# Second attention layer of a two-layer vision tower: gate shares from ScalarE's sigmoid, their products on GpSimd, a five-op cumulative step on VectorE

## What is computed

```
q, k, v, u = X @ Wq.T, X @ Wk.T, X @ Wv.T, X @ Wu.T          # per head
gate = X @ Wg.T                                               # per head: 3 numbers, two are used
s_i = -sum(u * (log_tau * prior_mu + cumsum(u)) / (log_tau + t)) / sqrt(d)
E_t = cumsum(exp(s_i - max(s_i)));  P_t = cumsum(s_i)
F_t, G_t, H_t = cumsum(exp_s * kv), cumsum(s_i * kv), cumsum(kv)
sig1, sigh = sigmoid(gate[0]), sigmoid(gate[1])
alpha = sigh / (E_t + 1e-12)
beta  = (sig1 - sigh) / t
gamma = -((beta * P_t + sigh) / t)
out = q @ (alpha * F_t + beta * G_t + gamma * H_t)            # then a layer norm per head, then Wo
```

## Time and profile before

| | |
|---|---|
| median of 3 runs | 573.85 us (572.05 to 574.06) |
| the profiled execution's own time | 573.22 us |
| its span, first to last instruction | 571.4 us |
| busy: PE / DVE / ACT / POOL | 519.4 / 382.5 / 255.6 / 225.8 us |
| mean granted clock of PE | 0.949 |

### The profile page before, as it was taken

One profiled execution on the slowest core, in us unless ns is written; L12 is line 12 of the kernel. 1 busy time (PEld: TensorE's weight loads), 2 busy tenths in 40 slices (PEclk: granted clock), 3 DMA queues, 4 the chain that ended last, 5 costly groups with the idle time before them and its releaser, 6 DMA issues.

```text
span 571.4 us, 9760 instructions
## 1 busy us (share of the span) xinstructions
PE 519.4 (91%) x3430; PEld 494.8 (87%) x3430; DVE 382.5 (67%) x923; ACT 255.6 (45%) x531; POOL 225.8 (40%) x186
## 2 busy tenths in 40 slices
PE   5799896989999999999999889897987779999996
PEld 5798895989999999999999779685766779999995
DVE  1575848756675667566654776899986765566665
ACT  0337562315544554455443236864641254253432
POOL 1403201746565676566667114374742200031300
PEclk9889959899999999999999989997988799799999
DMA  8750000947455775667653412000200200000001
GB/s 345 262 207 1 2 0 1 320 121 264 154 209 199 255 255 210 201 237 259 217 204 106 145 36 117 2 2 0 77 2 0 77 0 2 2 0 1 2 0 63
DMA packets 22635, 65.03 MB, mean 114 GB/s; under 512 B 6433, under 2 KB 15009, under 8 KB 19777
## 3 DMA queue, kind: packets, MB, share of 16 engines
q1 hardware_dynamic: 20192, 59.55, 29.7%
q0 software_dynamic: 2400, 4.93, 2.5%
HBM read 55.50 MB, written 8.97 MB: 113 GB/s over the span
## 4 chain that ended last, share of the span: by engine, by line
PE 60%; DVE 12%; DMA 2%; issue 2%; POOL 2%; ACT 2%; SPq 0%; DVEq 0%; POOLq 0%; ACTq 0%
PE psum L664 19%; PE psum L684 11%; PE psum L447 10%; PE psum L1073 4%; PE psum L464 3%; PE psum L1105 3%; PE psum L1088 2%; PE psum L471 2%; PE psum L1130 2%; DMA XR<-marked_rows 1%; DVE AT L2004 1%; PE psum L700 1%; PE psum L912 1%; DVE OW L1987 1%; DVE Y L1588 1%
## 5 line engine op out<-in xcount | busy, mean ns | idle before, releaser
L727 POOL TENSOR_TENSOR w0l<-stage,w0h 128x768 fp32r<-128x768 f32 x34 | 62.5, 1837 | 82.4 <-ACT w0h L711 70.9
L684 PE MATMUL psum<-w0d,a0h 128*128 128x192 f32 x492 | 84.7, 331 | 1.3 <-DVE a0h L766 1.3
L684 PEld LDWEIGHTS psum<-w0d,a0h 128*128 128x128 f32 x492 | 81.1, 193 | 1.6 <-DVE a0h L766 1.6
L759 DVE TENSOR_SCALAR a0t<-psum 128x256 f32<-128x256 f32 (+1 forms) x114 | 50.8, 445 | 42.6 <-PE psum L664 42.4
L738 ACT ACTIVATE psum<-psum 128x256 f32<-128x256 f32 x96 | 35.3, 368 | 85.3 <-PE psum L664 81.3
L664 PE MATMUL psum<-XWh,w0h 128*128 128x256 f32 x192 | 56.3, 293 | 0.0
L664 PE MATMUL psum<-XWh,w0t 128*128 128x256 f32 x192 | 54.4, 283 | 0.0
L664 PE MATMUL psum<-XWl,w0h 128*128 128x256 f32 x192 | 53.9, 281 | 0.0
L664 PE MATMUL psum<-XWh,w0l 128*128 128x256 f32 x192 | 53.9, 281 | 0.0
L664 PE MATMUL psum<-XWl,w0t 128*128 128x256 f32 x192 | 53.8, 280 | 0.0
L447 PE MATMUL psum<-X,w1h 128*128 128x384 f32 x144 | 49.5, 344 | 1.9 <-DVE a1hf L602 1.9
(11 more groups left out here) (258 smaller groups left out, 1296.7 us busy)
## 6 DMA issues: line engine op xcount, KB each, us to landing
stage<-moe0w SPq DMA_DIRECT2D x18, 1536.0 KB, 7.3
w0d<-moe0d SPq DMA_DIRECT2D x18, 576.0 KB, 3.9
stage<-moe1w SPq DMA_DIRECT2D x4, 1056.0 KB, 5.0
marked_rows<-zero SPq DMA_DIRECT2D x4, 772.0 KB, 12.9
patch<-patches SPq DMA_DIRECT2D x4, 768.0 KB, 7.9
XR<-marked_rows SPq DMA_DIRECT2D x16, 192.0 KB, 3.5
G<-slots_out SPq DMA_DIRECT2D x6, 288.0 KB, 4.7
XR<-marked_rows SPq DMA_DIRECT2D x16, 65.0 KB, 3.7
```

Of the source, the lines that this page charges most:

```text
L684: last = nc.tensor.matmul(dst, A0["h"][qpar][:, fc, t * P:(t + 1) * P], W0[par]["down"][:, fc, :], start=(fc == these[0]), stop=(fc == the ...
L727: ins = engine.tensor_tensor(W0[par]["l"][:, mat, :], src, W0[par]["h"][:, mat, :].bitcast(F32), ALU.subtract)
L759: nc.vector.tensor_scalar(A0["t"][fc % 2][:, 0:width], bank[2 + fc % 2][:, 0:width], LIMIT, -LIMIT, ALU.min, ALU.max).then_inc(S0["clip_re ...
```

## The change

- The sigmoid of batches 1 and 2 together (groups 4 to 10, 168 columns) is made by one ACT `Sigmoid`, straight into `SG`, in group 1 behind `exps(1)`. `exps(1)` and `exps(2)` no longer write `EG`.
- Batch 0 keeps exp, add 1 and reciprocal, but the last two stand in `first_sigmoids`, on DVE ahead of chain step 4.
- POOL makes beta, -sigh/t and -beta/t in four instructions (`share_factors`), ahead of `widen_values(0)` for batch 0 and in group 2 ahead of `rotate(3)` for the other two. The two products go into `EG`, which is free.
- The cumulative step is left with five DVE instructions. It waits for POOL by the new semaphore `l1_be`.
- `key_factors` makes `CK` in one instruction in place of two, `query_factors` makes `CQ` in one in place of three.

```diff
+                if g == 1:
+                    g0 = BATCHES[1][0]
+                    nc.scalar.activation(SG[:, g0:GROUPS, :], QK[:, g0:GROUPS, 4 * D:QKVG],
+                                         ACT.Sigmoid).then_inc(l1_sig, 1)
...
+            def share_factors(g0, g1):
+                be, s1, sh = CO[:, 1, g0:g1], SG[:, g0:g1, 0:HEADS], SG[:, g0:g1, HEADS:2 * HEADS]
+                shares.step(nc.gpsimd.tensor_scalar(EG[:, g0:g1, HEADS:2 * HEADS], sh, t_neg, None, ALU.mult))
+                shares.link(nc.gpsimd.tensor_tensor(be, s1, sh, ALU.subtract))
+                shares.link(nc.gpsimd.tensor_scalar(be, be, t_inv, None, ALU.mult))
+                nc.gpsimd.tensor_scalar(EG[:, g0:g1, 0:HEADS], be, t_neg, None, ALU.mult).then_inc(l1_be, 1)
...
-                    dve.wait_ge(l1_eg, j + 1)
-                    own.link(nc.vector.tensor_scalar(EG[:, g0:g1, :], EG[:, g0:g1, :], 1.0, None, ALU.add))
-                    own.step(nc.vector.reciprocal(sg, EG[:, g0:g1, :]))
-                    own.link(nc.vector.tensor_scalar(ga, cum[:, :, 0:HEADS], 1e-12, None, ALU.add))
-                    own.step(nc.vector.reciprocal(al, ga))
-                    own.link(nc.vector.tensor_tensor(be, s1, sh, ALU.subtract))
-                    own.step(nc.vector.tensor_tensor(al, al, sh, ALU.mult))
-                    own.link(nc.vector.tensor_scalar(be, be, inv_t, None, ALU.mult))
-                    nc.vector.tensor_tensor(ga, cum[:, :, HEADS:2 * HEADS], be, ALU.mult).then_inc(l1_read, 1)
+                    own.link(nc.vector.tensor_scalar(al, cum[:, :, 0:HEADS], 1e-12, None, ALU.add))
+                    own.link(nc.vector.reciprocal(al, al))
+                    dve.wait_ge(l1_be, min(j + 1, 2))
+                    own.step(nc.vector.tensor_tensor(al, al, SG[:, g0:g1, HEADS:2 * HEADS], ALU.mult))
+                    nc.vector.tensor_tensor(ga, cum[:, :, HEADS:2 * HEADS], EG[:, g0:g1, 0:HEADS],
+                                            ALU.mult).then_inc(l1_read, 1)
                     dve.wait_ge(l1_read, i + 1)
-                    own.link(nc.vector.tensor_tensor(ga, ga, sh, ALU.add))
-                    own.link(nc.vector.tensor_scalar(ga, ga, neg_inv_t, None, ALU.mult))
+                    own.link(nc.vector.tensor_tensor(ga, ga, EG[:, g0:g1, HEADS:2 * HEADS], ALU.add))
+            def first_sigmoids():
+                g1 = BATCHES[0][1]
+                dve.wait_ge(l1_eg, 1)
+                own.link(nc.vector.tensor_scalar(EG[:, 0:g1, :], EG[:, 0:g1, :], 1.0, None, ALU.add))
+                nc.vector.reciprocal(SG[:, 0:g1, :], EG[:, 0:g1, :]).then_inc(l1_rec, 1)
...
             norms(1)
+            first_sigmoids()
```

More of the change, by code:

```diff
@@ L315, in tower @@
             sem("l1_" + s) for s in ("mu", "cen", "csq", "var", "std", "hr", "on", "oT", "oTc", "f", "h"))
+        l1_rec, l1_sig, l1_share, l1_be = sem("l1_rec"), sem("l1_sig"), sem("l1_share"), sem("l1_be")
         stored = sem("stored")
@@ L1324, in exps @@
                 act.wait_ge(l1_out, 2 * g1)
-                nc.scalar.activation(EG[:, g0:g1, :], QK[:, g0:g1, 4 * D:QKVG], ACT.Exp, scale=-1.0).then_inc(l1_eg, 1)
+                if b == 0:
+                    nc.scalar.activation(EG[:, g0:g1, :], QK[:, g0:g1, 4 * D:QKVG], ACT.Exp,
+                                         scale=-1.0).then_inc(l1_eg, 1)
                 act.wait_ge(l1_read, CHAIN.index(("st", b)) + 1)
@@ L1542, in head_norm @@
                 pool.wait_ge(done, b + 1)
+            t_inv, t_neg = const[0:GW, C_RT:C_RT + 1], const[0:GW, C_NRT:C_NRT + 1]
+            shares = Steps(pool, l1_share)
+            def share_factors(g0, g1):
[4 more added lines that the diff above has]
+                nc.gpsimd.tensor_scalar(EG[:, g0:g1, 0:HEADS], be, t_neg, None, ALU.mult).then_inc(l1_be, 1)
             rotate(0)
             rotate(1)
+            pool.wait_ge(l1_rec, 1)
+            share_factors(*BATCHES[0])
             widen_values(0)
@@ L1553, in _ @@
                     head_norm(0, l1_hr, HR, ALU.mult, l1_on)
+                if g == 2:
+                    pool.wait_ge(l1_sig, 1)
+                    share_factors(BATCHES[1][0], GROUPS)
                 if j < len(PAIRS):
@@ L1924, in chain @@
                     cum = b[0:GW, 0:n * 2 * HEADS].rearrange("p (g h) -> p g h", h=2 * HEADS)
-                    al, be, ga = (CO[:, k, g0:g1] for k in range(3))
-                    sg = SG[:, g0:g1, :]
-                    s1, sh = sg[:, :, 0:HEADS], sg[:, :, HEADS:2 * HEADS]
-                    dve.wait_ge(l1_eg, j + 1)
-                    own.link(nc.vector.tensor_scalar(EG[:, g0:g1, :], EG[:, g0:g1, :], 1.0, None, ALU.add))
-                    own.step(nc.vector.reciprocal(sg, EG[:, g0:g1, :]))
-                    own.link(nc.vector.tensor_scalar(ga, cum[:, :, 0:HEADS], 1e-12, None, ALU.add))
-                    own.step(nc.vector.reciprocal(al, ga))
-                    own.link(nc.vector.tensor_tensor(be, s1, sh, ALU.subtract))
-                    own.step(nc.vector.tensor_tensor(al, al, sh, ALU.mult))
-                    own.link(nc.vector.tensor_scalar(be, be, inv_t, None, ALU.mult))
-                    nc.vector.tensor_tensor(ga, cum[:, :, HEADS:2 * HEADS], be, ALU.mult).then_inc(l1_read, 1)
-                    dve.wait_ge(l1_read, i + 1)
-                    own.link(nc.vector.tensor_tensor(ga, ga, sh, ALU.add))
-                    own.link(nc.vector.tensor_scalar(ga, ga, neg_inv_t, None, ALU.mult))
+                    al, ga = CO[:, 0, g0:g1], CO[:, 2, g0:g1]
+                    own.link(nc.vector.tensor_scalar(al, cum[:, :, 0:HEADS], 1e-12, None, ALU.add))
[4 more added lines that the diff above has]
+                                            ALU.mult).then_inc(l1_read, 1)
+                    dve.wait_ge(l1_read, i + 1)
+                    own.link(nc.vector.tensor_tensor(ga, ga, EG[:, g0:g1, HEADS:2 * HEADS], ALU.add))
[4 more added lines that the diff above has]
+                nc.vector.reciprocal(SG[:, 0:g1, :], EG[:, 0:g1, :]).then_inc(l1_rec, 1)
             def cosines(j):
@@ L1967, in key_factors @@
                 own.link(nc.vector.reciprocal(rn[o][:, 0:n, :], nrm[o][:, 0:n, :]))
[L1968 to L1971, removed]
+                nc.vector.tensor_tensor(
+                    CK[o][:, :, 0:n, :], ES[:, g0:g1, :].rearrange("p g (k h) -> p k g h", k=2),
+                    rn[o][:, 0:n, HEADS:2 * HEADS].unsqueeze(1).to_broadcast([GW, 2, n, HEADS]),
+                    ALU.mult).then_inc(l1_ck, 1)
             def query_factors(j):
@@ L1977, in query_factors @@
                 dve.wait_ge(l1_read, CHAIN.index(("cum", BATCH_OF[g0])) + 1)
[L1978 to L1981, removed]
+                own.link(nc.vector.tensor_tensor(
+                    CQ[o][:, 0:n].rearrange("p g h i -> p i g h"), CO[:, :, g0:g1, :],
+                    rn[o][:, 0:n, 0:HEADS].unsqueeze(1).to_broadcast([GW, 3, n, HEADS]), ALU.mult))
             def combine(g):
```

## The result

The changed kernel takes 563.74 us (median of 4 runs, 562.37 to 566.10) against 572.95 us for the kernel before (median of 4 in the same session, 569.18 to 574.06). The ratio is 0.9845, interval 0.9808 to 0.9882: 8.9 us faster, between 6.8 and 11.0. The forecast was 565.0 us.

What follows compares the result with a forecast made beforehand. VectorE was taken to pace the heads from the second cumulative step, level with PE before it. Terms 1.6 + 2.9 + 3.0 + 0.9 = 8.4 us off 573.22 gave 564.8, rounded up to 565.0 us; range 561.5 to 570.

Steps and rivals of the forecast that it cites:

- First step: First cumulative step (batch 0): add-one and reciprocal hidden in a wait for PE, 2.8 us falling to 1.2, gain 1.6 us.
- Second step: Second cumulative step: five instructions stay, two blocked by `widen_values` on GpSimd, 4.9 us falling to 2.0, gain 2.9 us.
- Third step: Third cumulative step: the same five instructions, 2.0 of 4.1 us, gain 2.1, plus 0.9 behind it, 3.0 us in all.
- The 0.9: Behind the third cumulative step: `head_O` ends before VectorE gets there, if PE keeps its clock, 0.9 us more.
- Joined factors: `CK` and `CQ` each made in one instruction: 0.4 us and 0.5 us over five times, 0.9 us in all.
- the 1.82 us: A `CQ` product as long as a GpSimd rotation addition; taken as a wait that stays, the joined one blocked likewise.
- rival B: Blocks fall away: joined `CQ(0)` slips ahead of the GpSimd addition, a later step loses its third block; 563 us, chance 0.14.
- ACT at nothing: ScalarE, group 1: second table load of 1.28 us and a 0.4 us sigmoid, ending at 372.2 under the old 372.66; no cost.
- POOL at nothing in group 2: GpSimd, group 2: four instructions of 84 columns, 1.3 to 2.35 us, delaying the rotation's addition 0 to 0.7; nothing on the path.
- rival A: Eight new GpSimd instructions each block a VectorE addition and later steps meet more blocks; gain 4.1 us, 569.1 us, chance 0.17.
- The 1.01 us row: Last instruction of the second cumulative step, 0.25 us in the first; taken as blocked by GpSimd, having two SBUF inputs.
- Sum: Whole heads: 8.4 us gained, with the masks of group 8 about 7.5 us earlier and the combine behind them 8.4.

Runs made afterwards that it cites:

- the kernel before with the step first: The kernel before with the second and third cumulative step put ahead of `key_factors` in groups 3 and 7, nothing else changed: 571.24 us, ratio 0.9951.
- the kernel with only the first step: The changed kernel with batches 1 and 2 back on the old ten instructions, `CK` and `CQ` still joined: 570.47 us, ratio 0.9990 to the kernel before.

## Why the prediction was right

- **First step, 1.6 us.** Mis-sized: 1.2. The two instructions were covered as said. The step with its links took 1.29 us, and behind it came an idle entry of 0.33 us. It stands behind the first step alone, in every kernel that has the new one, also where the step ended 1.2 us later, and what it waits for stays open. That GpSimd would be ready in time was right, with 0.66 us to spare where I had 0.8.
- **Second step, 2.9 us.** Right for the step: 4.84 to 1.92, including the two blocks at the first and second `widen_values`. By the kernel before with the step first, 2.06 us of the old step were waits and 2.78 work; now 0.63 are waits (1.92 less 1.29). So 1.5 of the 2.9 came from fewer instructions and 1.4 from fewer of them that can be blocked. What I had at nothing is that a wait moves on: the first addition of the combine of group 3 takes 0.88 us in all three traces of the changed kernel and 0.36 before, so 0.5 of the 2.9 was given back there.
- **Third step, 2.1 and 0.9 us.** The 2.1 was right (2.15). The 0.9 came (the combine gained 1.0 more than the masks), but not by the shorter step: with the old step and PE at full clock the wait is gone too, as the kernel with only the first step shows. My condition, that PE keeps its clock, is enough to explain all of it. That is a difference between executions, and luck in this sum.
- **Joined factors, 0.9 us.** Right in sum (0.94), wrong in one piece. I read the 1.82 us as the first `CQ` product; it is the third of pair 0, and the joined one was not blocked, as rival B had it. Most of what it won went into the wait for PE and the blocked addition.
- **ACT at nothing.** Right: the masks of group 2 stand at 14.8 with and without the second table load.
- **POOL at nothing in group 2.** Right in sum, wrong on the way there. The last of the four products took 1.50 us in two traces (0.67 in the third), the whole 3.0 in place of 2.35 at most, and `CQ` of pair 1 was blocked by the rotation's addition, which is rival A on a smaller scale. The same delay freed two other operations, and it came out even (1.29 us against 1.40). I had not seen either side.
- **What blocks.** The 1.01 us row that I gave as a case of two SBUF inputs is a scaling: one SBUF tile and a column of constants. And not every operation on SBUF data alone stands still: all 17 reciprocals of 96 columns take 0.75 us, whatever GpSimd does.
- **Sum.** At the masks of group 8 I had 7.5 us, and the three traces show 6.4, 6.7 and 7.0: the first step lacks 0.4, the combine of group 3 0.5. At the combine of group 7 I had 8.4, and they show 7.4, 7.7 and 8.0, of which 1.0 is the clock. In the first of them VectorE also waits twice for PE (0.25 and 0.83 us) behind the low clock stretch in the middle, which I had expected to go. It starts 35.97 us behind the product of pair 3 in place of 32.90; in the two other traces it is half as long (3.4 us in place of 6.8).
- **The number.** 563.74 against 565.0, and a ratio of 0.9845 against 0.9846, is closer than this can be known: the same kernel gave 0.9870 and 0.9777 in the two other sessions, 7.5 and 12.8 us. The size and the main terms were right, and the last microsecond was luck.
- The expert phase kept its length but for the clock: from `a1hl` to the end it is 111.5 us before and in two traces of the changed kernel, and 113.1 in the first one.

## What to carry to other kernels

Where an engine's queue has no gaps, count its instructions there as time, and price each as its row says while GpSimd is idle. Where GpSimd is busy, additions, products and scalings on SBUF data alone can cost the rest of its instruction on top. Moving small work to GpSimd paid here, where most of it ran while VectorE reduced, read PSUM or waited. Look at which long GpSimd instruction is pushed, for it can come to lie over another VectorE operation, or off one. An order in which the GpSimd work is released behind VectorE's short SBUF operations took 2.5 us out of the heads of the kernel before with no instruction changed, but 0.4 to 1.05 out of the changed one, whose two steps had only 0.6 and 0.7 us of waits left.

## What the runs showed that I had not expected

- A VectorE operation on one SBUF tensor and a constant can be blocked as long as an addition of two SBUF tensors: 1.79 us for the lower bound on 48 columns of norms, 0.18 free. The 143 products of the combine, which read PSUM, took 0.74 to 0.76 us in all traces. A reduction of 576 columns was never blocked (0.80 to 0.81 us each time), which also agrees with the Trainium skill (SBUF — State Buffer, Who interferes with whom), where a reduction on this chip does not contend.
- The stretches of PE's low clock come at other places in each execution. One at the output projections is worth 1.9 us (2.29 against 4.21 us), more than several of the edits tested.
- A GpSimd scaling of 48 columns takes 0.41 us and a subtraction of two tensors of that size 0.28.
